# Key rows of a stack in two transfers to 64 partitions, their source read twice, in place of four to 32

## The reference, cut to what matters

```python
x = x + 0.5 * ffn(layernorm(x))      # a shared expert and 8 routed ones, hidden size 128, the 2 best count
x = x + attn(layernorm(x))
x = x + 0.5 * ffn(layernorm(x))
# attn: 16 heads of 16 features, each query sees the last 64 keys
q, k, v = split_heads(x @ Wq), split_heads(x @ Wk), split_heads(x @ Wv)
scores = where(invalid, -inf, einsum('bhld,bhlwd->bhlw', q, k_win) * scale)
ctx = einsum('bhlw,bhlwd->bhld', softmax(scores), v_win);  out = ctx @ Wo
```

## Time and profile before

| | us |
|---|---|
| median of three runs | 1540.26 |
| profiled execution, its own time | 1536.15 |
| its span, first to last instruction | 1534.4 |
| TensorE busy (matmul) | 1498.8 (98%) |
| VectorE busy | 1158.8 (76%) |
| ScalarE busy | 1131.7 (74%) |
| GpSimd busy | 802.3 (52%) |
| DMA, mean over 16 engines | 45.5% for SP's queue (q1) |
| mean granted TensorE clock | 0.994 of full speed |

### The profile page before, as it was taken

The page is one execution under the profiler, slowest core; times in us unless marked ns, Lnnn a source line. Parts: engine busy times, 40 slices in busy tenths (PEclk is TensorE's granted clock), DMA queues, the critical chain, the costliest instruction groups (busy, mean ns, idle before and its releaser), DMA issues.

```text
span 1534.4 us, 41376 instructions
## 1 busy us (share of the span) xinstructions
PE 1498.8 (98%) x13953; PEld 1352.9 (88%) x13953; DVE 1158.8 (76%) x4773; ACT 1131.7 (74%) x3416; POOL 802.3 (52%) x794
## 2 busy tenths in 40 slices
PE   8999999999999999999999999999999999999898
PEld 7888889888998989899898988989898898989787
DVE  6767777868788786877868788786877878686664
ACT  5477787778777877777778677777877878677754
POOL 4445555546455554645546465554655556454443
PEclk9999999999999999999999999999999999999899
DMA  4175537264363735536363454726436362534410
GB/s 120 36 188 153 151 108 193 82 184 128 98 173 110 189 98 161 138 100 184 95 177 119 126 136 122 192 81 192 120 98 172 117 182 84 153 104 136 121 56 28
DMA packets 264392, 199.66 MB, mean 130 GB/s; under 512 B 150859, under 2 KB 220918, under 8 KB 264182
## 3 DMA queue, kind: packets, MB, share of 16 engines
q1 hardware_dynamic: 263972, 196.94, 45.5%
q0 software_dynamic: 32, 0.07, 0.0%
q10 hardware_dynamic: 178, 0.02, 0.0%
HBM read 141.86 MB, written 42.43 MB: 120 GB/s over the span
## 4 chain that ended last, share of the span: by engine, by line
PE 66%; DVE 11%; SPq 6%; issue 6%; ACT 4%; POOL 3%; DMA 3%; DVEq 0%; POOLq 0%; ACTq 0%
PE gb L1073 9%; PE gb L1075 8%; PE gb L1074 8%; PE yb L1073 7%; PE yb L1075 6%; PE yb L1074 6%; PE ptb L1151 5%; PE sb_ L1142 5%; PE cxb L1170 3%; SPq L587 3%; DMA gate<-gates_pair 2%; POOL gl L680 2%; PE gb L1192 2%; PE gb L1190 2%; SPq L582 2%
## 5 line engine op out<-in xcount | busy, mean ns | idle before, releaser
L680 POOL TENSOR_TENSOR gl<-ag,gh 128x512 fp32r<-128x512 f32 x288 | 387.5, 1351 | 306.4 <-ACT gh L783 302.6
L736 ACT ACTIVATE pr<-pr,mx 128x128 f32<-128x128 f32 x1024 | 397.1, 392 | 34.6 <-DVE mx L942 30.8
L663 POOL TENSOR_TENSOR pr<-pr,rinv 128x512 f32<-128x512 f32 x256 | 277.9, 1092 | 231.2 <-DVE rinv L950 229.9
L1073 PE MATMUL yb<-w2h,gh 128*128 128x256 f32 x1152 | 333.9, 290 | 3.5 <-POOL gl L680 3.1
L1075 PE MATMUL yb<-w2l,gh 128*128 128x256 f32 x1152 | 321.4, 279 | 0.0
L1074 PE MATMUL yb<-w2h,gl 128*128 128x256 f32 x1152 | 321.4, 279 | 0.0
L942 DVE CUSTOM_DVE_ANT_0 pr<-sb_,mask 128x128 f32<-128x128 f32 x1024 | 235.9, 285 | 72.2 <-PE ptb L1151 47.5
L798 ACT ACTIVATE tt<-gb,b1half 128x512 f32<-128x512 f32 x288 | 195.5, 680 | 119.3 <-PE gb L1075 104.9
L1073 PE MATMUL gb<-xh,w1h 128*128 128x512 f32 x576 | 241.7, 420 | 2.5 <-DVE ag L1014 2.0
L783 ACT ACTIVATE gh<-ag 128x512 fp32r<-128x512 f32 x288 | 178.7, 626 | 84.4 <-DVE ag L1020 50.8
L1014 DVE SCALAR_TENSOR_TENSOR ag<-gb,b,gate 128x512 f32<-128x512 f32 x256 | 188.6, 745 | 65.5 <-ACT tt L798 34.1
(11 more groups left out here) (159 smaller groups left out, 2792.3 us busy)
## 6 DMA issues: line engine op xcount, KB each, us to landing
gate<-gates_pair SPq DMA_DIRECT2D x240, 256.0 KB, 4.0
ks<-qk_dram SPq DMA_DIRECT2D x256, 128.0 KB, 2.8
qs<-qk_dram SPq DMA_DIRECT2D x512, 64.0 KB, 2.5
qk_dram<-qkh SPq DMA_DIRECT2D x64, 256.0 KB, 2.4
qk_dram<-qkl SPq DMA_DIRECT2D x64, 256.0 KB, 3.0
vb<-va SPq DMA_DIRECT2D x32, 384.0 KB, 7.4
xres<-L_attn_x_dram SPq DMA_DIRECT2D x16, 512.0 KB, 5.1
out_dram<-axn SPq DMA_DIRECT2D x16, 512.0 KB, 3.4
```

The costliest lines, as they stand in the source:

```text
L663: nc.gpsimd.tensor_tensor(pr[:, k], pr[:, k], rinv[:, k, :].unsqueeze(2).to_broadcast([P, NP, P]), ALU.mult).then_inc(a_pn, 1)
L680: nc.gpsimd.tensor_tensor(gl[:, k, :], ag[:, k, :], gh[:, k, :].bitcast(F32), ALU.subtract).then_inc(f_gl, 1)
L736: nc.scalar.activation(pr[:, k, r, :], pr[:, k, r, :], ACT.Exp, bias=mx[:, k, r:r + 1], scale=-1.0, accum_out=rsum[:, k, r:r + 1]).then_in ...
L1073: nc.tensor.matmul(dst, ah, bh, start=start, stop=False, **kw)
```

## The change

The keys' four transfers of a half stack become two. The first fills partitions 0 to 63 with the 32 rows of high parts, the second 64 to 127 with the low parts; each reads its 32 rows twice, by a source pattern with a leading dimension of size 2 and step 0. The number that the semaphore reaches for a half stack falls with the number of transfers, from 192 to 160. The eight transfers of the queries, the order of SP's steps and all else stay.

```diff
-        NSTK = 16 * 12
+        NSTK = 16 * 10
@@
                     ls = slice(hf * HL, hf * HL + HL)
-                    for part in range(4):
-                        sp.dma_start(ks[32 * part:32 * part + 32, :, ls].bitcast(F32), k_rows[c, part // 2, :, :, ls]) \
+
+                    for hl in range(2):
+                        sp.dma_start(ks[64 * hl:64 * hl + 64, :, ls].bitcast(F32),
+                                     k_rows[c, hl, :, :, ls].unsqueeze(0).to_broadcast([2, 32, NP, HL])) \
                             .then_inc(a_stk[hf], 16)
```

## The result

The changed kernel takes 1849.67 us (median of four runs, 1840.26 to 1857.06) against 1540.36 us before (also four runs), a ratio of 1.202 (1.199 to 1.205). The forecast was 1825 us, with a range of 1630 to 1940. The profiled execution took 1840.26 us, 304 us more than the one of before; its spans are 1838.5 and 1534.4.

The account below looks back on a forecast made before the run. TensorE, busy 1498.8 of 1534.4 us, was taken as the bound. Fourteen periods of 16.3 + 3 us (270) plus 16 for the last two gave +286, 1826 against the median, stated as 1825 us; range 1630 to 1940.

Parts of the forecast that it names:

- The number of engines: Key transfers: a source with outermost count 2 is carried by two engines, always the same two.
- The replay: Period of b = 8, work queued in order on the two engines: lateness grows to 16.3 us a period.
- S0: TensorE's score step that needs the period's first half stack: 2.3 us late.
- S4: TensorE's score step that first uses the second half stack: 6.1 us late.
- pa1: VectorE's first user of the first set of gates, queued behind the stack: its gate 8.9 us late.
- pa5: VectorE's first user of gates 5 to 8, behind the next half stack: its gate 16.3 us late.
- The clock: TensorE's lower clock after stalls: only loss after the late gates' last stall counts, 0 to 5 us a period, taken as 3.
- the last two periods: End of the run, few or no first-pass gates to wait for: stacks alone late, some 8 us each, 16 us.
- A: Rival: 16 engines still carry the new key transfers, nobody waits for the earlier stacks; 1536 to 1540 us, chance 0.08.
- B: Rival: two engines, but only the stack's readers are late, 6.1 us a period; 1638 us, chance 0.09.
- C: Rival: 16 engines, and earlier issues of stacks and gates bring a gain; 1521 to 1535 us, chance 0.03.
- D: Rival: every stall costs its clock too, or packets on two engines take longer; above 1940 us, chance 0.05.

Follow-up runs that it names:

- read4: Changed kernel with one key transfer per half stack, 32 rows of high parts read four times, low parts left out; 1615.66 us, ratio 1.053 to the kernel before.
- fill: Changed kernel with 18 and 36 identity matmuls on TensorE ahead of its waits for the two halves of c = 0; 1859.19 us, ratio 1.209 to the kernel before.
- only_c1: The change for the stacks of c = 1 alone, the four old transfers for c = 0; 1666.70 us, ratio 1.083 to the kernel before.
- read16: Changed kernel with one key transfer per half stack, 8 rows of high parts read 16 times, most key rows left out; 1531.05 us, ratio 0.996 to the kernel before.
- plain64: Changed kernel with each key transfer reading 64 different rows, so part of the keys are wrong; 1530.53 us, ratio 0.995 to the kernel before.
- pairs: Kernel before with key copies on neighbouring partitions and high and low query rows adjacent in DRAM, 8 issues a half stack; 1535.08 us, ratio 1.000.

## Why the prediction was right, step by step

**The number of engines** was read off the small packets of the earlier trace rows, and the small packets of five kernels follow the outermost count from 2 to 16.

**The price of a half stack**, 14.4 us on the two engines: the first query issue after the keys stood for 6.0 us, what one key transfer was priced at, and SP got from one half to the next in 933.27 - 919.23 = 14.0 us. The chain of the changed kernel in this period:

```profile
921.82 6.02 SPq L589
...
936.49 6.18 SPq L589
...
946.73 2.74 DMA qs<-qk_dram
```

**The replay**, all counted from the first key issue of the period (the earlier trace rows against the rows above):

| | before | after | late | forecast |
|---|---|---|---|---|
| S0 | 14.2 | 16.7 | 2.5 | 2.3 |
| S4 | 24.7 | 31.4 | 6.6 | 6.1 |
| pa1 | 27.1 | 38.1 | 10.9 | 8.9 |
| pa5 | 40.1 | 58.1 | 17.9 | 16.3 |
| next period's first key issue | 91.8 | 112.1 | 20.3 | 19.3 |

S0 agrees in part by luck: the first packet of the keys came 2.1 us after their issue (at 921.3), where the replay had 1 us, and S0 was only 0.2 us later than reckoned.

The step that failed inside it is that SP would be free 7.5 us after each start. It was held for 14, so the gates were issued 33.5 us after the start, where I had them issued early and waiting on the engines: about 2 us more at pa1, carried to pa5. Where the two engines are the bound it matters little who holds whom; read4, whose time came out 56 us above its range, is where it shows.

**The clock.** I took 3 us a period after qX1. The stretch at 0.50 there is one of 6.7 us:

```profile
977.40:984.10 6.70, 5.89 (x54) 5.53 (x55) 3.91 (x8) 1.12 (x2) 4.22 (x3) 0.50 0.34 102
```

With 5.9 us of busy time at half the rate that is 3 us of work lost, and by the table the period loses 2.4 us more after pa5 (20.3 - 17.9). The 96 us of slower matmuls over the run are not all on the path, as fill shows.

**The sum by stretches.** Key issues that begin the third period and the last but one, in the kernel before and in the changed one:

```profile
221.96 0.55 SPq L582 DMA_DIRECT2D ks<-qk_dram  x1
...
1315.72 0.55 SPq L582 DMA_DIRECT2D ks<-qk_dram  x1
```
```profile
260.75 2.45 SPq L583 DMA_DIRECT2D ks<-qk_dram  x2
...
1584.52 0.56 SPq L583 DMA_DIRECT2D ks<-qk_dram  x1
```

The first two periods brought 38.8 us (forecast 38.6) and the twelve after them 230.0, 19.2 each (forecast 19.3). The replay for b = 8 is 1.6 us short at pa5 and its 20.3 is above the twelve's mean, so part of that agreement is luck. The mis-sized term of the sum is the last two periods: 35.3 us where I had 16. I priced them at the stacks' lateness alone, 8 us each. In that stretch the waits for stacks come to 20.4 us at the matmuls, and a gate holds things up once more:

```profile
PE sb_ L1144 <- DMA qs<-qk_dram: 20.4, 4, 9.9
...
DVE ag L1016 <- DMA gate<-gates_pair: 12.5, 2, 7.8
...
PE gb L1075 <- DVE ag L1016: 6.9, 1, 6.9
```

That is 27 us of idle time, and 8 us more of busy time at the slower clock. The second pass's gates and the tighter stacks of the last sequence, which the steady period doesn't have, were not looked at.

**The rivals.** A (no change of the spread) is excluded by the packets. B (only the stacks' readers late, 1638 us) falls with only_c1, and with the 113 us that TensorE waits for banks behind the gates. C needed 16 engines; with them a gain was indeed there, 0.4 to 0.5% in read16 and plain64, but both leave part of the keys out, and pairs, which doesn't, gains nothing. D did not come: the rate on two engines was that of two engines.

One reading was loose: the 7.1 us of the earlier trace rows count the weight loads' idle time and the matmuls' idle time both; the matmuls' own is 3.2 us. In the changed kernel the matmuls' own is 97.6 us, within the 80 to 100 that I had put, but by the count of the earlier trace rows from which I had started it is 203.4 us, twice as much. The landings of 7 and 13 us that I named as a sign stand in no row of the changed kernel's profile.

## What to carry to other kernels

Look at the outermost dimension of both patterns of a transfer before joining transfers: a repeat of the source put outermost with a count of 2 leaves two engines to do the work, and the number of small packets in a window whose transfers are known tells how many engines each uses. A slow transfer has to be priced by what is queued behind it as well as by its own reader: in only_c1 the stacks came in time through twelve periods, and TensorE still stood still for 70.6 us behind the gates. And before a step is moved in a queue, list the waits that it carries with it.
